# Attention and expert outputs with tokens as rows, and norms shared by two engines

## The reference

```python
x = x + attention_a(norm(x))        # 16 heads, 64 wide, one key and value head shared by all, not causal
x = x + linear(norm(x))             # quantise_fp6(h) @ quantise_fp6(w).T + bias
x = x + attention_b(norm(x))        # 16 heads, causal
x = x + linear(norm(x))
x = x + latent_attention(norm(x))   # 16 heads, keys and values from a 32-wide latent, causal
x = x + experts(norm(x))            # router over 8 experts, 2 taken, and a shared expert
x = x + attention_c(norm(x))        # 16 heads, causal, with biases
x = x + experts(norm(x))
```

## Time and profile before

| what | us |
|---|---|
| median of 3 runs | 2778.26 (2777.01 to 2779.09) |
| the profiled execution | 2777.25 |
| its span, first to last instruction | 2775.5 |
| PE busy | 2530.6 (91%) |
| DVE busy | 1736.8 (63%) |
| POOL busy | 1237.8 (45%) |
| ACT busy | 1134.6 (41%) |

### The profile page before, as it was taken

One profiled execution on the slowest core, in us unless ns is written; L12 is line 12 of the kernel. 1 busy time (PEld: TensorE's weight loads), 2 busy tenths in 40 slices (PEclk: granted clock), 3 DMA queues, 4 the chain that ended last, 5 costly groups with the idle time before them and its releaser, 6 DMA issues. The chain is left out here.

```text
span 2775.5 us, 47142 instructions
## 1 busy us (share of the span) xinstructions
PE 2530.6 (91%) x19425; PEld 1243.0 (45%) x19425; DVE 1736.8 (63%) x2244; ACT 1134.6 (41%) x1454; POOL 1237.8 (45%) x810
## 2 busy tenths in 40 slices
PE   4999999889999999999994799998869999999968
PEld 2333344333334444444442466665434444444433
DVE  2677767777765766666657467775434666666653
ACT  1444444434444434444441244444214444444422
POOL 2677777666775444555550000000003555555510
PEclk9999999999999999999995699999868999999969
DMA  4000000000000000000000100000000000000000
GB/s 104 1 1 1 1 1 0 1 1 1 1 1 10 1 1 1 1 1 1 1 1 0 32 3 3 3 3 2 0 1 1 1 1 1 1 1 1 1 1 16
DMA packets 19321, 13.99 MB, mean 5 GB/s; under 512 B 3234, under 2 KB 17954, under 8 KB 18979
## 3 DMA queue, kind: packets, MB, share of 16 engines
q1 hardware_dynamic: 19106, 10.97, 1.6%
HBM read 9.39 MB, written 1.57 MB: 4 GB/s over the span
## 5 line engine op out<-in xcount | busy, mean ns | idle before, releaser
L1361 POOL TENSOR_TENSOR sums<-sums,p 128x1024 f32<-128x1024 f32 (+3 forms) x384 | 815.2, 2123 | 389.9 <-PE ps L1022 342.6
L1194 DVE TENSOR_REDUCE half_max<-ps 128x2 f32<-128x1024 f32 (+3 forms) x384 | 440.2, 1146 | 334.9 <-PE ps L1003 322.4
L1111 ACT ACTIVATE p<-ps 128x1024 f32<-128x1024 f32 (+3 forms) x384 | 347.8, 917 | 228.3 <-PE ps L982 163.3
L979 PE MATMUL ps<-q,k 64*128 64x512 f32 (+3 forms) x1792 | 428.0, 556 | 0.0
L772 POOL TENSOR_TENSOR sums<-sums,p 128x1024 f32<-128x1024 f32 (+3 forms) x160 | 276.9, 1731 | 196.1 <-PE ps L545 179.5
L1022 PE MATMUL ps<-p,v 128*64 128x512 f32 (+3 forms) x1536 | 343.8, 562 | 0.0
L982 PE MATMUL ps<-max_row,pick 64*128 64x512 f32 (+3 forms) x896 | 327.2, 726 | 0.0
L1214 DVE RECIPROCAL inverse<-total 128x128 f32<-128x128 f32 x256 | 240.0, 940 | 17.0 <-ACT total L1147 13.2
L1003 PE MATMUL ps<-k_near,q_near 64*128 64x512 f32 (+2 forms) x896 | 201.0, 445 | 51.8 <-DVE half_max L1194 51.7
L687 DVE TENSOR_REDUCE half_max<-ps 128x2 f32<-128x1024 f32 (+3 forms) x128 | 129.2, 1010 | 122.7 <-PE ps L526 107.5
L1003 PEld LDWEIGHTS ps<-k_near,q_near 64*128 64x128 f32 x896 | 85.9, 188 | 265.0 <-issue 157.2
(11 more groups left out here) (260 smaller groups left out, 3990.5 us busy)
## 6 DMA issues: line engine op xcount, KB each, us to landing
q_w<-in_wq SPq DMA_DIRECT2D x3, 512.0 KB
o_w<-in_wo SPq DMA_DIRECT2D x3, 512.0 KB
k_w<-in_wk SPq DMA_DIRECT2D x2, 512.0 KB
v_w<-in_wv SPq DMA_DIRECT2D x2, 512.0 KB
out<-x SPq DMA_DIRECT2D x4, 256.0 KB, 2.9
scratch<-in_wq_t SPq DMA_DIRECT2D x1, 512.0 KB, 5.4
scratch<-in_w_out SPq DMA_DIRECT2D x1, 512.0 KB, 7.6
gate<-in_gate SPq DMA_DIRECT2D x1, 320.0 KB
```

The source lines that it names most:

```text
L979: nc.tensor.matmul(out[:, head, 0:width], a.k[rows, owner(i) % 3, k * P:(k + 1) * P], a.q[rows, i % 3, s * BANK + lo:(s + 1) * BANK], star ...
L1111: act.activation(probabilities(g)[:, :, lo:BANK], score[g % 2][:, :, 0:BANK - lo], ACT.Exp)\
L1194: last = v.tensor_reduce(out, chunk_ps[:, :, 0:hi - lo], AX.X, ALU.max, negate=True)
L1361: pool.tensor_tensor(sums, sums, probabilities(g)[:, :, lo:BANK], ALU.add).then_inc(summed, 1)
```

## The change

- The output products of all attention layers take `mixed` as the stationary and the weight as the moving operand, in tiles of 128 tokens. The result has tokens on the partitions and is added straight to x. The clears of y_t go.
- The down product of the experts is turned round in the same way; VectorE adds the finished group to x.
- `norm_phase` has no transposes and adds of y. A new `shift` (minus mean times 1/std) lets ScalarE normalise groups 0 and 2; VectorE does groups 1 and 3.
- In the stream, "back" is gone, the "evens" are on ScalarE, and all offsets are moved.
- In the biased layer the bias is a row, put into the bank by a product with a row of ones in the first pair of heads of each batch.
- `final_phase` is gone; the second `moe_phase` stores each group when it is added.

```diff
-def norm_phase(nc, m, tag, add, linear=False):
+def norm_phase(nc, m, tag, linear=False):
...
-            if add:
-                for g in range(GROUPS):
-                    for t in range(TPG):
-                        at = g * BANK + t * P
-                        last = nc.tensor.transpose(m.ps[:, g, t * P:(t + 1) * P], m.y_t[:, at:at + P], m.ident[:])
-                    last.then_inc(y_back, 1)
...
                 link(nc.vector.reciprocal(rstd[:], var[:]))
+                nc.vector.scalar_tensor_tensor(shift[:], mv[:, :, 0], -1.0, rstd[:], ALU.mult, ALU.mult)\
+                    .then_inc(shift_ready, 1)
...
+                act.wait_ge(shift_ready, n + 1)
+                for g in range(0, GROUPS, 2):
+                    if n:
+                        act.wait_ge(turned, g + 1)
+                    for t in range(g * TPG, (g + 1) * TPG):
+                        last = nc.scalar.activation(xn[:, t, :], m.x[:, t, :], ACT.Identity, bias=shift[:, t:t + 1],
+                                                    scale=rstd[:, t:t + 1])
+                    last.then_inc(normed[0], 1)
...
                     pe.wait_ge(normed, unit(i, part) + 1)
-                    last = nc.tensor.matmul(small, w.o[:, i // B, :], a.mixed[:], start=True, stop=True)
+                    with_bias = biased and i // B == 0
+                    if with_bias:
+                        nc.tensor.matmul(small, m.ones_row[:], a.y_bias[:], start=True, stop=False)
+                    for t in range(TPG):
+                        last = nc.tensor.matmul(small[:, t * P:(t + 1) * P], a.mixed[:, t * P:(t + 1) * P],
+                                                w.o[:, i // B, :], start=not with_bias,
+                                                stop=not with_bias or t == TPG - 1)
...
-        NORM_USES = {("back", 0): 2, ("back", 1): 4, ("turn", 0): 39, ("turn", 1): 41, ("line", 0): 43, ("line", 1): 45,
-                     ("turn", 2): 54, ("turn", 3): 56}
-        NORM_DVE = {("stats", 0): 4, ("stats", 1): 6, ("gather", 0): 8, ("invert", 0): 9, ("even", 0): 10,
-                    ("even", 1): 11, ("stats", 2): 45, ("stats", 3): 47, ("gather", 1): 48, ("invert", 1): 50,
-                    ("even", 2): 51, ("even", 3): 52} | {("quantise", n): 12 + n for n in range(26)}
-        NORM_ACT = {("root", 0): 8, ("root", 1): 49}
+        NORM_USES = {("turn", 0): 36, ("turn", 1): 38, ("line", 0): 40, ("line", 1): 42, ("turn", 2): 51, ("turn", 3): 53}
+        NORM_DVE = {("stats", 0): 2, ("stats", 1): 3, ("gather", 0): 5, ("invert", 0): 6, ("stats", 2): 42,
+                    ("stats", 3): 44, ("gather", 1): 45, ("invert", 1): 47} | {("quantise", n): 9 + n for n in range(26)}
+        NORM_ACT = {("root", 0): 5, ("even", 0): 7, ("even", 1): 8, ("root", 1): 46, ("even", 2): 48, ("even", 3): 49}
...
+            def make_even(n, part):
+                base = norms[n][1] * BT
+                act.wait_ge(shift_ready, 2 * n + part // 2 + 1)
+                if part >= 2:
+                    act.wait_ge(small_mm, use_of["turn", n, part - 2] + 1)
+                for t in range(part % 2 * TPG, part % 2 * TPG + TPG):
+                    last = act.activation(even_tiles[:, t, :], m.x[:, base + t, :], ACT.Identity, bias=shift[:, t:t + 1],
+                                          scale=rstd[:, t:t + 1])
+                last.then_inc(even_ready, 1)
...
-                nc.tensor.matmul(m.ps[:, 6, :], m.down[:, c, :], hid[:, i % 2, :], start=c == 0,
-                                 stop=c == shared).then_inc(downed, 1)
+                for t in range(TPG):
+                    last = nc.tensor.matmul(m.ps[:, 6, t * P:(t + 1) * P], hid[:, i % 2, t * P:(t + 1) * P],
+                                            m.down[:, c, :], start=c == 0 and t == 0, stop=c == shared,
+                                            skip_group_check=True)
+                last.then_inc(downed, 1)
...
+            def add_experts(g):
+                dve.wait_ge(downed, (g + 1) * CHUNKS)
+                x = m.x[:, g * TPG:(g + 1) * TPG, :]
+                v.tensor_tensor(x, x, m.ps[:, 6, :].rearrange("p (t d) -> p t d", d=D), ALU.add).then_inc(summed_out, 1)
...
+                if c == 0 and g >= 1:
+                    add_experts(g - 1)
+            add_experts(GROUPS - 1)
-def final_phase(nc, m, out):
```

More of the change, by code:

```diff
@@ L339, in _ @@
                              quantised)
-                add_and_measure(product, 1)
-            for g in range(GROUPS):
+                measure(True, 1)
+            for g in range(1, GROUPS, 2):
                 normalise(g)
@@ L913, in stream_phase @@
             if n + 1 < len(layers) and pair == PAIRS - 1:
-                norms.append((begins[i] + when(i)["out", 1], b))
-        uses += [(start + at, kind, n, part) for n, (start, _) in enumerate(norms)
+                norms.append((begins[i] + when(i)["out", 1], b, i))
+        uses += [(start + at, kind, n, part) for n, (start, _, _) in enumerate(norms)
                  for (kind, part), at in NORM_USES.items()]
@@ L921, in stream_phase @@
             uses_at.setdefault(g, []).append((n, kind, i, part))
-        for n, (start, _) in enumerate(norms):
+        for n, (start, _, _) in enumerate(norms):
             for (kind, part), at in NORM_DVE.items():
@@ L1172, in _ @@
                 for one in (g, g + 1):
-                    for _, n, part in act_at.get(one, ()):
-                        root(n, part)
+                    for kind, n, part in act_at.get(one, ()):
+                        if kind == "root":
+                            root(n, part)
+                        else:
+                            make_even(n, part)
         @block.vector
@@ L1241, in norm_work @@
                 if kind == "stats":
-                    dve.wait_ge(small_out, use_of["back" if part < 2 else "line", n, part % 2] + 1)
+                    first = use_of["line", n, part % 2] if part >= 2 else use_of["out", norms[n][2], part % 2]
+                    dve.wait_ge(small_out, first + 1)
                     for t in range(part % 2 * TPG, part % 2 * TPG + TPG):
@@ L1253, in norm_work @@
                     link(v.reciprocal(rstd, var))
[L1254 to L1257 removed]
+                    v.scalar_tensor_tensor(shift, mv[:, :, 0], -1.0, rstd, ALU.mult, ALU.mult).then_inc(shift_ready, 1)
+                elif part < 24:
                     if part < 2:
[L1259 to L1262 removed]
+                        dve.wait_ge(even_ready, 4 * n + part + 1)
                     link(quantise_step(part // 2, part % 2), behind=1)
@@ L1554, in use_small @@
                     pe.wait_ge(normed, unit(i, part) + 1)
-                    last = nc.tensor.matmul(small[:, 0:QW], w.o[:, i // B, :], a.mixed[:, 0:QW], start=True, stop=True)
+                    for t in range(2):
+                        last = nc.tensor.matmul(small[:, t * P:(t + 1) * P], a.mixed[:, t * P:(t + 1) * P],
+                                                w.o[:, i // B, :], start=True, stop=True)
                 last.then_inc(small_mm, 1)
@@ L1737, in routed_before, with _ @@
             return i - i // CHUNKS
+        if out is not None:
+            @block.sync
+            def _(sp):
+                for g in range(GROUPS):
+                    tiles = slice(g * TPG, (g + 1) * TPG)
+                    sp.wait_ge(summed_out, g + 1)
+                    sp.dma_start(out.rearrange("(t p) d -> p t d", p=P)[:, tiles, :], m.x[:, tiles, :])\
+                        .then_inc(stored, 16)
+                sp.wait_ge(stored, 16 * GROUPS)
         @block.tensor
```

164 lines of the change are left out of this document (59 added, 105 removed).

## The result

The changed kernel took 2739.34 us (median of four timed runs, 2724.3 to 2742.12) against 2777.64 before: ratio 0.9853, interval 0.9822 to 0.9883. The forecast was 2751.0, with a range of 2735 to 2772. Before, runs lie within 4 us of each other; after, within 18. The profile of after is the fastest of its runs (2724.3, span 2722.6), so a second one belongs beside it: the same kernel, run again, took 2741.45 in its profiled execution (span 2739.7). Both are read here.

The account below looks back on a forecast made before the run. Bounds: TensorE's own time in full stretches, VectorE's chain in norm phases, the late row maximum in mixed stretches. Terms +3 -1 +5.2 -17 -3.9 +4.4 -18 = -27.3 take 2777.25 to 2750.0, median 2751.0 us; range 2735 to 2772.

Parts of the forecast that it names:

- rival D: Stream norms: whole gross gain arrives and one lost clock less brings the next; -30 instead of -18, 2739 us; 19%.
- Term 2: Expert loop: turned down product takes 1.09 instead of 0.96 us, 40 times; +5.2 us, bounds 0 and +10.
- Term 5: Biased layer: bias sum on one row +0.5, four bias products +3.9; +4.4 us, bounds -2 to +5.
- Term 6: Norms inside the attention stream: normalising to ScalarE, no way back; gross -27, net -18 us, bounds -32 and +5.
- Term 1: Attention output products turned round: +0.03 us each for 96 units (+3), latent layer -1; bounds -5 to +8.
- Term 3: Norm phases: statistics earlier without y's return, splitting the normalisation worth nothing; -17 us, bounds -21 and -10.
- the 5.35 us of the estimate: Norm phases: split normalisation and transposes with shift and an extra hop, against 5.36 before; nothing gained a pass.
- Term 4: Kernel's end: one add and its store replace ScalarE's copy and four adds; -3.9 us, bounds -5 and -2.
- Rival B: Stream norms: the late row maximum only moves, so that term gives nothing; 2769 us; 18%.
- that sign: Mixed stretches: TensorE's waits for the row maximum under 15 us over both; staying near 30 would refute.
- the three waits priced there: Stream norms: TensorE's stands for the late row maximum of 3.16, 5.05 and 4.38 us.
- rival C: Turned products: freshly written stationary tiles hide no load, six added loads stand open; +118 us, 2869; 2%.

Follow-up runs that it names:

- kernel 2: Changed kernel with the old stream in the first two attention layers and y's way back there and in n2; 2761.05 us.
- kernel 4: Changed kernel with all its new stream work put back at the old offsets, ScalarE still normalising; 2735.16 us.
- kernel 5: Against kernel 4: VectorE instead of ScalarE normalises in the stream, at the old offsets, without y's way back; 2751.63 us.
- kernel 6: Against kernel 2: the stream's normalising moved to ScalarE at the same old offsets, y's way back kept; 2743.98 us.
- kernel 9: Changed kernel with the norm phases normalised wholly on VectorE, without shift, the stream still on ScalarE; 2739.01 us.
- kernel 8: Changed kernel with unused identity transposes in TensorE's waits in the norm phases n2, n3, n4 and n5; 2737.57 us.
- kernel 12: Changed kernel with old offsets, VectorE's groups first in the norm phases, and 36 unused transposes in n3 and n5; 2728.03 us, ratio 0.9817.
- the six: Six profiles of one stream, the changed kernel's with ScalarE normalising at the new offsets; its two norm-carrying stretches took 659.8 to 665.7 us, mean 663.7.

## Why the prediction was right, point by point

The mechanism of its largest term is shown by kernels 2, 4, 5 and 6, but 2739 is rival D's number and not the forecast's 2751, which is 12 too high. Part of the total is luck: terms 2, 5 and 6 were each priced too high, and in eight of the thirteen profiles a slow latent start (72.4 to 74.8 us), which the sum does not have, took some of that back. Where that start went well (2724.3) the time lies below the range.

- **Term 1, output products.** Right: +0.03 each (eleven units 250.17 to 250.54). The latent pair gained nothing: 0.64 for four tiles against 0.63 before (1586.46 to 1587.09), +0.4 over the layer instead of -1.
- **Term 2, expert product.** Too dear. I took 1.09 from the value projection; it is 0.99, and a step grew from 3.19 to 3.24 (1982.30 to 1985.54): +2 for 40 steps instead of +5.2. Behind the value projection stood a value product, behind the expert product the spread; whether that makes the 0.10 wasn't tried.
- **Term 3, norm phases.** Aggregation after the last out 4.0 us earlier in n2, n3 and n5 (the table), n2's pairs 1.25, n4 3.4 (from the last down product: 2025.95 to 2037.25, now 1985.54 to 1993.47). The split, put at nothing, costs 0.2 in n3 (8.69 to 8.92; kernel 9 has the same 0.2 in n2 and n5): the 5.35 us of the estimate had the tile at 0.37 where ScalarE takes 0.40. n2 went from 8.34 to 8.92, but before's transposes ran there at a clock of 0.56, so 0.4 of it is clock. Some -16 instead of -17.
- **Term 4, tail.** From where ScalarE's copy or VectorE's add starts to the end of the span: 8.71 before, 3.94 now: -4.8 instead of -3.9.
- **Term 5, biased layer.** The four bias products cost 1.05 each, as forecast, and the bias sum 0.4 more. Not seen: the start of the layer is 5.5 and 5.2 us shorter, and 4 to 6 in every variant but kernel 8. TensorE's first projections take 1.13 us there where they took 2.08. The clock is higher behind the sixteen v_bias products, which are now 128 columns wide instead of 1. Width alone doesn't bring it: kernel 8 has the same wide products, and its first projections still took 2.08. Kernel 8 also has fillers ahead of them; the cause stays open. So about -1.5, the outs' 0.9 set aside, instead of +4.4.
- **Term 6, the norms in the stream.** The size was off, not the mechanism: -18 forecast, -25.4 and -28.6 measured once the outs' +0.9 is set aside, between the forecast and rival D. At the old offsets the normalising gives 16 to 21, net of ScalarE's own delay (forecast 20 less 4), and the way back 4 to 8.5 (forecast 7). So at the old offsets the gain, ScalarE's delay taken off, was 28.4 (687.5 to 660.0, and 0.9 for the outs) where the forecast has 23, and the 5 that I charged for quantising at other steps was 4, if kernels 4 and 12 against the six are taken at their word. Rival B, in which the late row maximum only moves, falls: the waits went from 30.3 to 18.8 us. I had asked for under 15, and that sign failed. It asked for more than the sum has: the three waits priced there are 12.6 us, and 11.5 went. What was more is clock, priced at 9.3 and measured at 13: over 480-680 and 860-1060 us the 100 us windows have 0.95, 0.97, 0.95 and 0.93 before, 0.98, 1.00, 0.98 and 0.97 after, 13 us of full clock in 400.
- **The rule on VectorE's ports.** The Trainium skill (SBUF — State Buffer, "Who interferes with whom") says that GpSimd and VectorE's 2-port modes lock each other out, and that ScalarE has ports of its own. Both halves agree with the traces: 4.57 against 1.11 us for VectorE, 3.18 against 3.19 for ScalarE, and single tiles of 2.38 us that end with POOL's add.
- **The rule on weight loads.** The sentence of the Trainium skill (TensorE: Matmul & The Clock Gate, "The mechanism") that the prediction goes by would have left six loads a product open; the same section also lets a load go ahead that targets the background weight buffer, which the prediction leaves out. The output product takes 1.09 us with eight: rival C falls. The runs don't show where the loads go.
- **What hid in the sum.** The forecast took the starts of the stages as fixed. The latent start alone is -4.5 in one profile and +5.9 in the other. By stretches the profile of again sums to -35.8, 8.5 more than forecast: term 6 some 7, term 5 some 5, term 2 some 3 and the tail 1 more, less some 5 for the slow latent start and 3 for small items.

## What to carry to other kernels

A cheap VectorE step can be the dearest in a stream if it falls beside GpSimd's adds: look at one operation's duration in two places before pricing it, and either move it in time or give it to ScalarE. A size taken from one profile holds the clock of that profile; where a stage starts in TensorE's slow level, keep 10 us of either sign beside the sum. When work is split between two engines, the group that the next engine waits for first belongs to the faster one (0.65 us a pass here).

## What the runs showed of the hardware that was not expected

- One kernel's executions on one chip differ by 10 us through the clock at one stage start (64.4 to 74.8 us for the same instructions). In the two mixed stretches the same code lost 6.8 to 13.7 us of full clock in six profiles, which is why their sum spreads from 659.8 to 665.7.
- TensorE kept busy with transposes in n2 had full clock for much of it and at its end, and still 0.50 in the next stage, whose first products stand 0.5 to 1.5 us apart. What decides between 0.88 and 0.50 in the first 12 us of that stage stays open.
- Eight weight loads are hidden whatever tile is loaded: 1.09 us for eight 128-column matmuls with `mixed`, written 4.3 to 5.5 us earlier in most plain units, and with normed tokens that had long been there.
- VectorE's tiles beside GpSimd's adds are held until the add ends (2.38 us, against 0.34 for the one between two adds), while the adds take 2.35 to 2.41 us with VectorE or ScalarE beside them.
